# Later slots for rounding the query weight of cross-attention, and a later fetch of half the output weight

## The reference

```
x1  = layernorm1(x);  q, k, v = split(x1 @ sa_wqkv)
sa  = softmax(causal(q k^T / sqrt(512))) v @ sa_wproj + sa_bproj
r   = x + sa
q2  = layernorm2(r) @ ed_wq;   k2, v2 = split(layernorm2(ctx) @ ed_wkv)
ca  = softmax(q2 k2^T / sqrt(512)) v2 @ ed_wproj + ed_bproj
out = r + ca + relu(layernorm3(x) @ ff_w1 + ff_b1) @ ff_w2 + ff_b2
```

## Time and profile before

| | |
|---|---|
| median of 3 runs | 1360.51 us (1359.99 to 1362.99) |
| the profiled execution: its time | 1362.29 us |
| the profiled execution: span of the records | 1359.6 us |
| TensorE busy | 1302.6 us, 96% |
| VectorE, ScalarE, GpSimd busy | 790.8, 665.8, 699.3 us |
| mean granted TensorE clock | 0.992 |

### The profile page before, as it was taken

How to read it: one execution, slowest core, us unless ns; L and a number is a source line. 1 busy time by engine, 2 the same in 40 slices (tenths; PEclk the granted TensorE clock), 3 DMA queues, 4 the chain that set the end, 5 groups by cost and what they waited for, 6 DMA issues and landing times.

```text
span 1359.6 us, 24602 instructions
## 1 busy us (share of the span) xinstructions
PE 1302.6 (96%) x9193; PEld 1078.2 (79%) x9193; DVE 790.8 (58%) x2003; ACT 665.8 (49%) x1611; POOL 699.3 (51%) x582
## 2 busy tenths in 40 slices
PE   6999999999999999999898999999999999999997
PEld 6888888888878888888687787877878787887874
DVE  6613223232677777767655575756657575575575
ACT  5411111231665766656625556574655647456444
POOL 3232131322444664548643767575676766667661
PEclk9999999999899999999999999999999999999999
DMA  7400102114557585687567666768667577766641
GB/s 238 142 24 16 62 32 70 54 47 121 133 149 197 145 194 141 164 217 195 166 119 133 115 94 116 131 112 146 92 135 117 99 130 120 130 101 107 93 70 41
DMA packets 102128, 160.06 MB, mean 118 GB/s; under 512 B 10389, under 2 KB 63421, under 8 KB 100730
## 3 DMA queue, kind: packets, MB, share of 16 engines
q1 hardware_dynamic: 102010, 158.50, 55.5%
HBM read 70.93 MB, written 28.31 MB: 73 GB/s over the span
## 4 chain that ended last, share of the span: by engine, by line
PE 78%; DVE 6%; POOL 6%; DMA 3%; issue 3%; ACT 3%; SPq 1%; POOLq 0%; DVEq 0%; ACTq 0%
PE ps L1772 19%; PE ps L453 12%; PE ps L164 11%; PE ps L423 10%; PE ps_pair L1789 6%; PE ps L1804 5%; PE ps L1818 5%; PE ps L1881 3%; POOL ca_partial L1634 2%; DMA ca_k_stack<-ca_keys 2%; POOL ca_xT L1516 2%; PE ps L1244 1%; PE ps L1836 1%; PE ps_pair L1234 1%; PE ps L1264 1%
## 5 line engine op out<-in xcount | busy, mean ns | idle before, releaser
L1711 DVE TENSOR_REDUCE ca_maxes<-ps 112x1 f32<-112x375 f32 x512 | 258.4, 548 | 112.4 <-PE ps L1804 110.4
L1655 ACT ACTIVATE ca_probT<-ps_pair 125x448 f32<-125x448 f32 x384 | 211.1, 556 | 181.0 <-PE ps_pair L1789 179.6
L1634 POOL TENSOR_TENSOR ca_partial<-ca_partial,ca_probT 125x896 f32<-125x896 f32 x118 | 249.4, 2113 | 93.3 <-ACT ca_probT L1655 88.7
L312 POOL TENSOR_TENSOR ff_hT<-ff_hrelu,ff_hT 128x512 fp32r<-128x512 f32 (+1 forms) x64 | 78.8, 1232 | 203.4 <-DVE ff_hT L394 203.4
L1804 PE MATMUL ps<-ca_k_stack,ca_q_stack 96*112 96x376 f32 x512 | 167.8, 351 | 6.8 <-DVE ca_maxes L1711 4.0
L1789 PEld LDWEIGHTS ps_pair<-ca_q_stack,ca_k_stack 98*125 98x125 f32 x768 | 130.7, 187 | 44.0 <-issue 31.9
L1789 PE MATMUL ps_pair<-ca_q_stack,ca_k_stack 98*125 98x224 f32 x768 | 156.7, 286 | 1.3 <-ACT ca_probT L1655 1.1
L423 PE MATMUL ps<-ff_w,ff_hT 128*128 128x512 f32 x672 | 155.5, 390 | 0.0
L1772 PE MATMUL ps<-ca_xT,w_a 128*128 128x376 f32 x768 | 154.6, 337 | 0.4 <-ACT ca_xT_f L1698 0.4
L1772 PE MATMUL ps<-w_b,ca_xT 128*125 128x512 f32 x576 | 149.6, 396 | 2.4 <-POOL ca_xT L1516 2.4
L423 PEld LDWEIGHTS ps<-ff_w,ff_hT 128*128 128x128 f32 x672 | 125.6, 188 | 25.8
(11 more groups left out here) (144 smaller groups left out, 2424.0 us busy)
## 6 DMA issues: line engine op xcount, KB each, us to landing
ca_k_stack<-ca_keys SPq DMA_DIRECT2D x96, 376.0 KB, 8.0
sa_Q_stack<-sa_rows SPq DMA_DIRECT2D x96, 112.0 KB, 3.7
sa_K_stack<-sa_rows SPq DMA_DIRECT2D x96, 112.0 KB, 3.8
ca_q_stack<-q_out SPq DMA_DIRECT2D x96, 112.0 KB, 9.5
ctx_tokens<-in_ctx_dram SPq DMA_DIRECT2D x14, 672.0 KB
ctx_tokens<-in_L_xattn_ff_w_dram SPq DMA_DIRECT2D x16, 512.0 KB, 4.3
q_out<-sa_yT SPq DMA_DIRECT2D x16, 448.0 KB, 4.0
wp_lo<-wp_out SPq DMA_DIRECT2D x6, 1024.0 KB, 4.8
```

The costliest lines, as they stand in the source:

```text
L312: pool.tensor_tensor(hT[:, LO, m % RING, 0:width(g)], hrelu[i % 2][:, 0:width(g)], hT[:, HI, m % RING, 0:width(g)].bitcast(F32), ALU.subtr ...
L1634: pool.tensor_tensor(total, total, half(a), ALU.add).then_inc(partial_done, 1)
L1655: act.activation(probT[u // GH][0:JT, u % GH].rearrange("p a t -> p (a t)"), ps_p[u % 2][0:JT, 0:2 * T], ACT.Exp).then_inc(exp_done, 1)
L1711: dve.tensor_reduce(maxes[:, q, j, a:a + 1], ps_s[n % 3][0:TQ, 0:JH], AX_X, ALU.max).then_inc(s_read, 1)
```

## The change

Half 0 of `ed_wq` is rounded in slot 8 and half 1 in slot 13, instead of slots 3 and 5. The first half of `ed_wproj` is fetched in slot 15 instead of 12, and rounded in slot 18 instead of 17. Nothing else differs.

```
-Y_WEIGHTS = [3, 5]
-PREPARED_WEIGHTS = [(12, 17), (24, 29), (36, 45), (54, 61), (70, 77), (86, 93)]
+Y_WEIGHTS = [8, 13]
+PREPARED_WEIGHTS = [(15, 18), (24, 29), (36, 45), (54, 61), (70, 77), (86, 93)]
```

## The result

The changed kernel takes 1366.38 us (median of 9 runs, 1363.64 to 1369.12), against 1360.33 for the kernel before in the same rounds (9 runs, 1359.15 to 1363.73). The ratio is 1.0041 with a 95% interval of 1.0028 to 1.0054: slower by 0.41%. The prediction was 1358.9 with a range up to 1362.0, so the sign was wrong and the result lies outside the range. The profiled execution took 1366.85 us, its span is 1364.1.

What follows compares the result with a forecast made beforehand. TensorE was taken to bound the kernel. Gains of 1.50 and 3.09 (or 1.56) against losses of 0.15, 1.26 and perhaps 1.56 gave a middle of -1.6 us from 1360.51: 1358.9 us, range 1356.2 to 1362.0.

Steps and rivals of the forecast that it cites:

- What bounds the kernel: TensorE, busy 96% of the span, no other engine above 58%; time can be won only where it idles or runs slowly.
- Slots 3 to 9, the start of Q(1,0): Without the weight's rounding in slots 3 and 5, Q(1,0) starts at about 351.39 instead of 352.89: gain 1.50 us.
- After 1.9 us idle instead of 3.37 I take it to stay up: Behind slots 6 and 7, TensorE's clock stays at its higher level: gain 3.09 us, bounds 0 and 3.09.
- the term of 3.09: From 352.89 to 359.79, two products and four head steps take 3.81 us at full clock instead of 6.90.
- The second rival: "The stall only changes its name": clock falls anyway after slots 6 and 7, 1.50 gained, 1.4 lost again; 1360.4 to 1362, 8%.
- Slots 8 and 9 at no cost: Half 0's rounding there takes 1.03 us on ScalarE and 1.22 to 1.58 on VectorE, and costs TensorE 0.
- Slots 13 to 17: Half 1's keep delays the masks for GpSimd about 1.1 us, so head 16's scores slip: loss 0.15, bounds 0 and 0.6.
- The moved fetch: Issued at 378.0, landing after 5.0 us at 383.0, ScalarE waits about 4.3; P(0,0) loses 1.26 us, bounds 0.4 and 3.5.
- The path from the landing to P(0,0), L + 4.8: From landing L, 2.9 us to head 20's masking, then 1.90 to P(0,0), at 387.8 instead of 386.54.
- the cover: In slots 18 and 19 the two V products cover most of ScalarE's 4.3 us wait, leaving a loss of 1.26.
- The clock ahead of P(0,0): About 2.5 us of idle TensorE there may bring the lower clock: another 1.56 us lost, bounds 0 and 3.09.
- Slower, by the moved fetch alone: Rival: fetch lands after 7.2 us, 3.5 lost plus a 3.09 clock fall ahead of P(0,0), against 3.06 gained: 1364.2, 8%.

Runs made afterwards that it cites:

- residual_early: The changed kernel with bias (224 KB) and residual rows (448 KB) of batch 0 fetched in slot 5 instead of 12; ratio 1.0016 to the kernel before.
- the runs of the halves: Against the kernel before: query weight rounded in slots 8 and 10, fetch untouched, 0.9990 and again 0.9986; only the fetch moved to 15 and its rounding to 18, 1.0039.
- both_away: The changed kernel with batch 0's bias and residual fetched in slot 5 and feed-forward's 448 KB in slot 19; ratio 1.0016 to the kernel before.
- round_at_21: The changed kernel, but what is fetched in slot 15 is rounded in slot 21 instead of 18; 1361.59 us against 1359.64 for the kernel before, ratio 1.0009.
- round_at_21b: Second run of the kernel with rounding in slots 8, 13 and 21; 1361.21 us against 1360.27 for the kernel before, ratio 1.0004.

## Why the prediction was wrong, point by point

- *What bounds the kernel:* right. Both places named, slots 6 and 7 and P(0,0), are where the times part.
- *Slots 3 to 9, the start of Q(1,0):* "Gain 1.50" was mis-sized; 0.62 was measured (351.92 and 0.35, against 352.89). ScalarE's half came out (transposes forecast at 348.77, measured 348.38 + 0.35). VectorE's half did not, since I took the split's 0.62 us over without asking what GpSimd would do next to it: it took 0.97, and the `sa_rinv` copy ahead of it 0.52 instead of 0.29. The value product came at 350.99 on the old clock instead of 350.43.
- *"After 1.9 us idle instead of 3.37 I take it to stay up":* this step failed. 2.3 us idle was left, and the clock fell to its lower level again, from 350.4 to 357.2. 11 of the 12 profiles with the rounding out of slots 3 to 5 show such a fall. So the term of 3.09 was 0.64 (1.26 - 0.62) in this pair of traces, and nothing that can be put down to the change, since the fall's length differs as much from trace to trace. The second rival was the true course of this part. The earlier trace rows had shown a fall after 1.64 us; I had used that row for P(0,0) and not here.
- *Slots 8 and 9 at no cost:* right, no idle TensorE from 351.92 to 371.4.
- *Slots 13 to 17:* the mechanism was right (keep, masks, GpSimd, head 16's maxima), its size 0.67 instead of 0.15. The upper bound of 0.6 was nearer.
- *The moved fetch, "I take 5.0, since 512 KB less is in flight before it":* this is the larger step that failed. The place in the queue was right (forecast issue 378.0, measured 377.26 on a clock 0.9 to 1.6 earlier). The landing was 7.7. The argument gave too much to the 512 KB that are missing ahead of it: `residual_early` took 672 KB away there, and that saved 0.9 us. The queue is full from 366 on in the changed kernel, and the stacks and the residual still stand ahead of the fetch. In the trace that I read, the queue had room until about 372 (shares of 0.55 to 0.75), which no other trace repeats. The rows showed neighbours at 5.9 and 7.2, and I had put the nearest of them, 7.2 us for 448 KB issued directly behind, into the rival with 8%. It should have been the main value. The sign hung on both failed steps: with the first part at 1.26 and the fetch as forecast the sum is +0.15 or +1.7, and with the fetch as measured and the rest as forecast it is +1.9 or +3.5. By the runs of the halves, the rounding is worth -1.4 to -1.9 us (forecast -3.1 to -4.6) and the fetch +5.4 (forecast +1.3 to +2.8).
- *The path from the landing to P(0,0), L + 4.8:* right. 377.26 + 7.7 + 4.8 = 389.8, measured 389.63. So was the cover: 4.3 - 1.26 = 3.04 forecast, 3.1 measured.
- *The clock ahead of P(0,0):* the fall came, and cost 2.34, between the 1.56 and the 3.09 of the text.
- *Which case came:* "Slower, by the moved fetch alone", the landing about as described there (7.7 for 7.2) and a fall of 2.34 for 3.09, at +3.7 instead of the measured +6, mostly because it had counted a gain of 3.06 in the first part that was 1.26. The Trainium skill (DMA: Bandwidth & Descriptors, Rules for kernel authors) says to issue a DMA early and to wait for it late, and the trace agrees that this move goes the wrong way: ScalarE waits 7.1 us. To charge that wait whole would be too much by the cover, since P(0,0) is late by 4.0.

What stays open: what slot 13 costs beyond the 0.66 us seen, why the stacks fill the engines at 150 GB/s in most traces and not in that of the kernel before, and why `residual_early` and `both_away` stay 2 us above the kernel before with P(0,0) not late; their new waits of 1.25 us are seen in one execution each and were not tried apart.

## What to carry to other kernels

A DMA that is moved to the tail of a busy queue is priced by when the queue runs empty, not by its landing time in a quiet place. The DMA share by stretch shows that, but of one execution, and here the one that was read was the odd one. Then ask which engine waits for it in order, and how many microseconds of that wait the bottleneck's own work covers, since only what is beyond counts. When a stall is shortened but not removed, look at what fills the time next (here GpSimd beside VectorE), and don't book the clock as won. And two edits whose sum is a loss should be tried apart: here one half is worth about -0.1%, which is hardly clear of noise, and the other +0.4%.

## What the runs showed of the hardware

Stacks of 896-byte rows kept the DMA engines full at 140 to 166 GB/s in `both_away` (370 to 380). The same stacks passed at 156 to 181 GB/s with the engines 0.55 to 0.62 busy in the kernel before (366 to 370), in bursts of some 300. In a queue full of them a 512 KB fetch took 6.0 us, against 3.8 to 4.1 in quiet places.

VectorE's 0.62 us subtraction took 0.97 when GpSimd's had begun before it. When VectorE's began first, GpSimd's step took 0.91 instead of 0.56. A copy of VectorE's went from 0.29 to 1.32 us beside GpSimd's bias addition (`residual_early`).

TensorE's clock fell behind the waits of 0.69 and 1.57 us in 11 of 12 profiles, and not in the twelfth, `round_at_21`. `round_at_21b` is the same program with the same two waits, and there it fell (2.85 us for the Q product instead of 1.58). Behind waits of 0.4 to 0.75 us ahead of the first V product it fell in 7 of 14.
